# Softmax denominators of an attention stage: 32x32 transposes and column halvings in place of products with ones

## The chip, the cores and the metric

The kernel runs on one core of a Trainium2 chip. The metric is the device time of one execution in microseconds (us). Engines: TensorE (PE; its weight loads are PEld), VectorE (DVE), ScalarE (ACT), GpSimd (POOL) and SyncE (SP), which issues most transfers. Each runs its own instructions in order, and they wait for one another by semaphores.

## The reference

Four stages over 4 sequences of 1024 rows of 256 values: a mixing attention, an expert layer, causal attention with 16 heads of 64, and the expert layer again. The change is in the causal attention:

```python
q = jnp.einsum('ntc,hdc->nhtd', x_q, w_q)
k = jnp.einsum('ntc,hdc->nhtd', x_q, w_k)
v = jnp.einsum('ntc,hdc->nhtd', x_q, w_v)
a = jnp.einsum('nhtd,nhsd->nhts', q, k) / math.sqrt(q.shape[3])
a = jnp.where(causal_forbidden[None, None], -jnp.inf, a)
a = jax.nn.softmax(a, axis=3)
y = jnp.einsum('nhts,nhsd->nthd', a, v).reshape(a.shape[0], t, -1)
return y @ w_o
```

## The kernel before

**Units and iterations.** Attention works through 32 units u (4 sequences times 8 pairs of heads). A unit has two chunks c of 512 queries. Chunk 0 has key tiles kt 0 to 3, chunk 1 kt 0 to 7 (128 keys each), so a unit is six iterations of two key tiles: two for chunk 0, four for chunk 1. `attend(u)` writes them out and hands over, at numbered places, to the work of the next unit (projections, row maxima), which the engines take in between. The order on each engine is the order of this text.

**What a key tile passes through.** PE multiplies keys and queries into two PSUM banks, one for each head (`high_scores` L1411, `scores` L1427). ACT takes the exponential into a buffer `t_p` (L1713; there are four). On the diagonal POOL zeroes the forbidden half (`affine_select`, L2370; the mask). One iteration later PE multiplies the weights with the values (`weigh` L1446, both heads into bank 6), and POOL adds the tile to the chunk's sum `t_acc` (`add_up` L2390, 128 keys x 2 heads x 512 queries; L2387 copies what the next tile leaves out). `weigh` of a diagonal tile waits for its mask. ACT copies the finished sum of values to `t_pvs` (L1731).

**The denominators.** `t_acc` still has to be summed over its 128 partitions. `divide` (L1456) multiplies it with 64 columns of ones, 512 columns a head, so that 64 partitions a head hold the same denominators. `sum_rows` on DVE transposes that bank in 32x32 blocks (L2204), inverts one column of each block (L2206), and `scale_rows` turns the inverses back to rows (L2213); POOL multiplies them into `t_pvs` and writes `t_yT` (L2404), which the output products (L1471) read. The chunk that ended with iteration n-3 is divided in `finish(n)`, ahead of that iteration's `weigh`, and scaled one iteration later. So chunk 1 of unit u-1 is divided in iteration 2 of unit u (below: den A), and chunk 0 of unit u in iteration 4 (den B). The first sum of a chunk in the next unit waits until PE has read the old one.

**Row maxima of the next unit.** PE multiplies whole blocks (`row_max` L1376, L1389) and DVE takes the maxima (`part_max` L2180 with the mask, L2186 without), which frees the banks. Seven banks go round in turn (`work_ring`) for scores, maxima, projections and denominators; PE takes a bank only when it has been drained. In iteration 1 DVE has masked maxima of 384 and 512 columns, then in iteration 2 of 128 and 256, then plain ones of 512 in two lots of four, one of them at the end of iteration 3.

Of the kernel before, what the change touches and what calls it, by code (L numbers as in the profile page):

```python
# [15 lines left out]
P = 128  # L16
# [32 lines left out]
class Kernel:  # L49
# [34 lines left out]
    def semaphores(self):  # L84
# [38 lines left out]
        self.pe_pv, self.a_pvs, self.p_yt = s("pe_pv"), s("act_pvs"), s("pool_yT")  # L123
        self.d_den = Marks(s("dve_den"), "reciprocal", "rows")

# [14 lines left out]
    def constant_tiles(self, st):  # L140
# [105 lines left out]
    def attention_tiles(self, st):  # L246
# [35 lines left out]
        t["wo"] = sb("t_wo", [P, NHP, D])  # L282
        t["den"] = [sb("t_den", [P, BANK]) for _ in range(2)]
        t["rden"] = [sb("t_rden", [P, BANK // 32]) for _ in range(2)]
# [107 lines left out]
class Program:  # L392
# [30 lines left out]
    xt_block = qk_load = v_load = qk_product = qk_low = qk_double = v_product = skip  # L423
    row_max = part_max = max_rows = high_scores = scores = weigh = add_up = divide = sum_rows = scale_rows = skip
    values_done = out_weights = out_load = out_product = out_add = skip
# [303 lines left out]
    def attention(self):  # L729
# [77 lines left out]
        def sums(n, *tiles):  # L807

            if 0 < n <= len(pairs):
                u, c, kt = pairs[n - 1]  # L810
                for i in tiles:
                    self.add_up(u, c, kt + i)

        def finish(n):

            if ends(n - 3):
                self.divide(*pairs[n - 3][:2])
            if 0 < n <= len(pairs):
                u, c, kt = pairs[n - 1]
                self.weigh(u, c, kt)  # L820
                self.weigh(u, c, kt + 1)
            if ends(n - 3):
                self.sum_rows(*pairs[n - 3][:2])
            if ends(n - 4):
                scale(*pairs[n - 4][:2])
# [135 lines left out]
        def units():  # L961
# [60 lines left out]
class TensorE(Program):  # L1022
# [711 lines left out]
class VectorE(Reader):  # L1734

    def constants(self):
# [453 lines left out]
    def max_rows(self, u):  # L2190
# [4 lines left out]
        dve.tensor_scalar(t["neg"][u % 2][:], k.bank[bank][0:2 * k.NBLK, 0:P], -1.0, None, ALU.mult).then_inc(k.drained[bank], 1)  # L2195

    def sum_rows(self, u, c):
# [3 lines left out]
        den = t["den"][c]  # L2201
# [3 lines left out]
        self.wait_drained(("den", u, c))  # L2205
        dve.reciprocal(t["rden"][chunk % 2][:, :], den[:].rearrange("p (n j) -> p n j", j=32)[:, :, 0]  # L2206
                       ).then_inc(k.d_den.sem, 1)

    def scale_rows(self, u, c):
        k, dve, t = self.k, self.e, self.k.t  # L2210
        chunk = 2 * u + c
        self.wait_ge(k.d_den.sem, k.d_den.at(chunk, "reciprocal"))
        dve.transpose(t["den"][c][:], spread(t["rden"][chunk % 2][:], 2, 32)).then_inc(k.d_den.sem, 1)  # L2213

# [8 lines left out]
class GpSimd(Reader):  # L2223
# [149 lines left out]
    def add_up(self, u, c, kt):  # L2373
# [16 lines left out]
        pool.tensor_tensor(acc[:, :, q0:], (p0 if kt == 1 else acc)[:, :, q0:], p[:, :, q0:],  # L2390
                           ALU.add).then_inc(k.p_acc, 1)

    def scale_rows(self, u, c):
# [10 lines left out]
        pool.tensor_tensor(t["yT"][c][:, hp, :], t["pvs"][chunk % 2][:], t["den"][c][:],  # L2404
                           ALU.mult).then_inc(k.p_yt, 1)
# [236 lines left out]
```

## Time and profile before

| | us |
|---|---|
| median of 3 runs (2241.84 to 2243.07) | 2243.05 |
| span of the profiled execution | 2235.8 |
| PE busy | 2149.9 (96%) |
| DVE busy | 1465.4 (66%) |
| POOL busy | 1368.7 (61%) |
| attention stage, from its first unit to its last den | 644 to 1804 |

The span runs from the first to the last instruction; 7.25 us lie around it. The busy share of an engine is a mean over stages. In the timelines a row is a start, a duration, an engine, a line and an operation with the tiles that it writes and reads; in brackets stands how long the engine had been idle, and for whom. A duration of PE is modelled and overlaps the next one, so the work of PE is better read from starts and from the chain of waits.

### The profile page before, as it was taken

The page shows a single profiled execution, that of the slowest core. Times are in us where ns is not written, and L with a number is a line of the kernel's source. Part 1 is how long each engine was busy: PE and PEld are TensorE (multiplying, and loading weights), DVE is VectorE, ACT ScalarE, POOL GpSimd, SP SyncE. Part 2 cuts the span into 40 slices and gives each one's busy share as a digit, 9 for nine tenths or more (in the row PEclk, how much of TensorE's full clock was granted, in tenths as well). Part 3 has the DMA queues.
Part 4 walks back from the last instruction along what each step waited for, and adds up shares of the span by engine and source line. Part 5 has one row for each costly group of instructions (what it writes and reads, how often), then busy time and mean ns, then how long its engine had stood idle before and what let it go on. Part 6 is the DMA issues. An engine that isn't in the chain of part 4 may idle for free.

```text
span 2235.8 us, 34077 instructions
## 1 busy us (share of the span) xinstructions
PE 2149.9 (96%) x12130; PEld 1597.8 (71%) x12130; DVE 1465.4 (66%) x3349; ACT 1003.6 (45%) x1907; POOL 1368.7 (61%) x1237
## 2 busy tenths in 40 slices
PE   6998999999999999999999999999999899999997
PEld 5455788889876666766657666667666588889997
DVE  6365688675757666467674577874877636975553
ACT  4411553444445545345553354542554425434443
POOL 2322676677537776566674576664677846777774
PEclk9899999999999999999999999999999999999999
DMA  4432544555432212212312222221220244545552
GB/s 132 144 129 86 151 117 111 151 144 137 114 88 67 51 36 76 67 52 73 76 48 67 67 78 56 58 61 54 76 76 21 76 132 115 140 113 139 134 144 29
DMA packets 145048, 206.04 MB, mean 92 GB/s; under 512 B 19432, under 2 KB 112112, under 8 KB 144880
## 3 DMA queue, kind: packets, MB, share of 16 engines
q1 hardware_dynamic: 120304, 170.30, 25.4%
q0 software_dynamic: 24576, 33.57, 8.8%
q8 instruction: 97, 1.59, 0.3%
q14 instruction: 71, 0.58, 0.1%
HBM read 130.03 MB, written 39.85 MB: 76 GB/s over the span
## 4 chain that ended last, share of the span: by engine, by line
PE 73%; DVE 9%; issue 4%; POOL 4%; ACT 2%; DMA 1%; SPq 1%; POOLq 0%; DVEq 0%; ACTq 0%
PE psum L1299 12%; PE psum L1320 11%; PE psum L1446 11%; PE psum L1348 7%; PE psum L1411 7%; PE psum L1427 6%; PE psum L1471 5%; PE psum L1362 4%; PE psum L1376 3%; PE psum L1456 3%; POOL t_acc L2390 2%; DVE f_hlo L2134 1%; DVE f_hhi L2132 1%; PE psum L1389 1%; PE psum L1267 1%
## 5 line engine op out<-in xcount | busy, mean ns | idle before, releaser
L1713 ACT ACTIVATE t_p<-psum 128x512 f32<-128x512 f32 (+3 forms) x768 | 323.6, 492 | 294.3 <-PE psum L1427 284.6
L2390 POOL TENSOR_TENSOR t_acc<-t_acc,t_p 128x1024 f32<-128x1024 f32 (+3 forms) x256 | 416.9, 1629 | 14.5 <-ACT t_p L1713 0.5
L2309 POOL TENSOR_TENSOR f_wlo<-f_wst,f_whi 128x256 fp32r<-128x256 f32 x256 | 221.8, 922 | 150.6 <-ACT f_whi L1646 150.6
L1320 PE MATMUL psum<-f_whi,f_hhi 128*128 128x256 f32 x1024 | 294.9, 288 | 6.2 <-DVE f_hlo L2134 6.1
L1446 PE MATMUL psum<-t_p,t_v 128*64 128x512 f32 (+3 forms) x1536 | 288.8, 496 | 7.3 <-POOL t_p L2370 7.3
L1320 PE MATMUL psum<-f_whi,f_hlo 128*128 128x256 f32 x1024 | 289.4, 283 | 0.0
L1320 PE MATMUL psum<-f_wlo,f_hhi 128*128 128x256 f32 x1024 | 289.2, 282 | 0.0
L2132 DVE CAST f_hhi<-f_h 128x512 fp32r<-128x512 f32 x256 | 141.9, 554 | 208.0 <-ACT f_h L1664 153.2
L1664 ACT ACTIVATE f_h<-psum 128x512 f32<-128x512 f32 x256 | 153.0, 598 | 275.8 <-PE psum L1299 246.8
L1411 PE MATMUL psum<-t_qa,t_ka 128*128 128x512 f32 (+3 forms) x768 | 222.7, 370 | 1.8 <-DVE t_mx L2180 0.6
L2390 POOL TENSOR_TENSOR t_acc<-t_p 128x768 f32<-128x768 f32 x64 | 134.6, 2103 | 136.4 <-PE psum L1456 133.1
L1446 PEld LDWEIGHTS psum<-t_p,t_v 128*64 128x64 f32 x1536 | 98.9, 137 | 161.8 <-issue 143.8
L2370 POOL TENSOR_SCALAR_AFFINE_SELECT t_p<-t_p 128x256 f32<-128x256 f32 x256 | 105.0, 420 | 175.0 <-ACT t_p L1713 174.5
L1299 PE MATMUL psum<-f_xhi,f_whi 128*128 128x512 f32 x512 | 204.8, 400 | 7.4 <-DVE f_xlo L2118 3.8
L1427 PE MATMUL psum<-t_qb,t_kb 65*128 65x512 f32 (+3 forms) x768 | 205.8, 349 | 4.9 <-DMA t_qb<-t_neg 4.5
L2134 DVE TENSOR_TENSOR f_hlo<-f_h,f_hhi 128x512 fp32r<-128x512 f32 x256 | 200.3, 783 | 8.8
L1320 PEld LDWEIGHTS psum<-f_whi,f_hhi 128*128 128x128 f32 x1024 | 194.9, 190 | 15.0 <-DVE f_hlo L2134 8.1
L1299 PE MATMUL psum<-f_xlo,f_whi 128*128 128x512 f32 x512 | 201.9, 394 | 0.0
L1299 PE MATMUL psum<-f_xhi,f_wlo 128*128 128x512 f32 x512 | 200.9, 392 | 0.0
L1320 PEld LDWEIGHTS psum<-f_wlo,f_hhi 128*128 128x128 f32 x1024 | 195.2, 191 | 4.8
L1320 PEld LDWEIGHTS psum<-f_whi,f_hlo 128*128 128x128 f32 x1024 | 195.0, 190 | 0.0
L2186 DVE TENSOR_REDUCE t_mx<-psum 128x1 f32<-128x512 f32 x256 | 159.6, 683 | 41.5 <-PE psum L1376 38.9
(288 smaller groups left out, 4408.1 us busy)
## 6 DMA issues: line engine op xcount, KB each, us to landing
f_wst<-in_L_ffn_w SPq DMA_DIRECT2D x64, 1024.0 KB
t_ka<-t_ka SPq DMA_DIRECT2D x64, 256.0 KB, 3.3
t_qb<-t_qa SPq DMA_DIRECT2D x64, 256.0 KB, 4.0
t_wk<-wkT SPq DMA_DIRECT2D x32, 256.0 KB, 4.0
t_wq<-wqT SPq DMA_DIRECT2D x32, 256.0 KB, 4.0
t_wv<-wvT SPq DMA_DIRECT2D x16, 512.0 KB, 4.9
normal<-f_xy SPq DMA_DIRECT2D x5, 1024.0 KB, 10.3
a_x<-in_L_attn_a_x SPq DMA_DIRECT2D x4, 1024.0 KB, 10.0
```

What stands on the lines that cost most here:

```text
L1299: m = pe.matmul(k.bank[b], w[:, dt, fs], x[:, dt, :], start=(dt == 0 and j == 0), stop=(dt == k.DT - 1 and j == 2))
L1320: m = pe.matmul(out, h[:, js], w[:, f, :], start=(f == 0 and a == 0 and j % 2 == 0), stop=(f == FT - 1 and a == 2), skip_group_check=True)
L1348: m = pe.matmul(k.bank[bank], w[:, part, ct, :], x[:, ct, cs], start=(ct == 0 and a == 0), stop=(ct == 1 and a == 2))
L1411: pe.matmul(k.bank[bank][:, q0:], hd["ka"][:, ks], hd["qa"][:, qs], start=True, stop=False)
L1427: pe.matmul(k.bank[banks[i]][:, q0:], hd["kb"][0:k.QROWS, ks], hd["qb"][0:k.QROWS, qs], start=False, stop=True).then_inc(k.filled[banks[i] ...
L1446: m = pe.matmul(k.bank[6][i * DH:(i + 1) * DH, q0:BANK], v[:, kt, vs:vs + DH], p[:, i, q0:BANK], start=(kt == 0), stop=(kt == last), skip_ ...
L1713: act.activation(p[:, i, q0:], k.bank[bank][:, q0:], ACT.Exp, scale=1.0 / float(np.sqrt(k.DH))).then_inc(k.drained[bank], 1)
L2132: dve.tensor_copy(hhi[:], h[:]).then_inc(k.d_h.sem, 1)
L2134: dve.tensor_tensor(hlo[:], h[:], hhi[:].bitcast(F32), ALU.subtract).then_inc(k.d_h.sem, 1)
L2186: s = dve.tensor_reduce(mx1[:, i, n - k.KPC:n - k.KPC + 1], part, AX.X, ALU.max)
L2309: m = pool.tensor_tensor(t["wlo"][n % 2][:, i, ks], t["wst"][:, i, ks], t["whi"][n % 2][:, i, ks].bitcast(F32), ALU.subtract)
L2390: pool.tensor_tensor(acc[:, :, q0:], (p0 if kt == 1 else acc)[:, :, q0:], p[:, :, q0:], ALU.add).then_inc(k.p_acc, 1)
```

## The change

The partition sum is made in three steps. `fold_sums` on DVE transposes the whole sum `t_acc`, 128 x 1024, in 32x32 blocks into a new tile `t_turned`; now each partition holds, for one query of a block, 32 keys in 32 columns. `fold_sums` on POOL adds these 32 columns in five halvings in place (16, 8, 4, 2 and 1 columns of each of the 32 blocks), the last into `t_part` (128 x 32); each waits for the one ahead of it. `divide` then multiplies `t_part` with `fold` (a matrix that adds the four groups of 32 partitions), 16 columns a head, and DVE inverts those 16 columns straight out of PSUM. The rows of inverses go into one half of `t_turned`, so the tile is shared: DVE may turn a new sum into it only once POOL has multiplied with the last rows (`p_yt`).

The order changes as well: `fold_sums` stands at the start of the iteration, and `divide` behind that iteration's `weigh`.

```diff
@@ tiles
-        t["den"] = [sb("t_den", [P, BANK]) for _ in range(2)]
+        t["turned"] = sb("t_turned", [P, 2 * BANK])
+        t["den"] = [t["turned"][:, c * BANK:(c + 1) * BANK] for c in range(2)]
+        t["part"] = sb("t_part", [P, 2 * BANK // 32])
@@ attention()
+        def fold(n):
+            if ends(n - 3):
+                self.fold_sums(*pairs[n - 3][:2])
         def finish(n):
-            if ends(n - 3):
-                self.divide(*pairs[n - 3][:2])
             if 0 < n <= len(pairs):
                 u, c, kt = pairs[n - 1]
                 self.weigh(u, c, kt)
                 self.weigh(u, c, kt + 1)
             if ends(n - 3):
+                self.divide(*pairs[n - 3][:2])
                 self.sum_rows(*pairs[n - 3][:2])
@@ attend(u)
+                fold(n)
                 sums(n, 0)
@@ TensorE.divide
-        self.wait_ge(k.p_acc, k.sum_count(u, c, k.KPC * (c + 1) - 1))
+        self.wait_ge(k.p_fold, 5 * (2 * u + c + 1))
         for i in range(2):
-            m = pe.matmul(k.bank[bank][i * DH:(i + 1) * DH, :], k.ones[:, 0:DH], t["acc"][(2 * u + c) % 2][:, i, :],
+            m = pe.matmul(k.bank[bank][i * DH:(i + 1) * DH, 0:n], k.fold[:], t["part"][:, i * n:(i + 1) * n],
@@ VectorE
+    def fold_sums(self, u, c):
+        self.wait_ge(k.p_acc, k.sum_count(u, c, k.KPC * (c + 1) - 1))
+        if chunk:
+            self.wait_ge(k.p_yt, chunk)
+            self.wait_filled(("den", (chunk - 1) // 2, (chunk - 1) % 2))
+        dve.transpose(t["turned"][:], t["acc"][c][:].rearrange("p i q -> p (i q)")).then_inc(k.d_den.sem, 1)
     def sum_rows(self, u, c):
-        if chunk > 1:
-            self.wait_ge(k.p_yt, chunk - 1)
-        dve.transpose(den[:], k.bank[bank]).then_inc(k.drained[bank], 1)
-        dve.reciprocal(t["rden"][chunk % 2][:, :], den[:].rearrange("p (n j) -> p n j", j=32)[:, :, 0]
+        dve.reciprocal(t["rden"][chunk % 2][:, :], k.bank[bank][:, 0:BANK // 32]).then_inc(k.drained[bank], 1)
@@ GpSimd
     def add_up(self, u, c, kt):
             if u:
-                self.wait_filled(("den", u - 1, c))
+                self.wait_ge(k.d_den.sem, k.d_den.at(2 * (u - 1) + c, "turned"))
+    def fold_sums(self, u, c):
+        rows = t["turned"][:].rearrange("p (n j) -> p n j", j=32)
+        self.wait_ge(k.d_den.sem, k.d_den.at(chunk, "turned"))
+        if chunk:
+            self.wait_filled(("den", (chunk - 1) // 2, (chunk - 1) % 2))
+        for n, w in enumerate((16, 8, 4, 2, 1)):
+            if n:
+                self.wait_ge(k.p_fold, 5 * chunk + n)
+            out = rows[:, :, 0:w] if w > 1 else t["part"][:].unsqueeze(2)
+            pool.tensor_tensor(out, rows[:, :, 0:w], rows[:, :, w:2 * w], ALU.add).then_inc(k.p_fold, 1)
```

The order on POOL from the scaling of chunk 1 of the last unit (`t_yT`) to that of chunk 0, iterations 3 to 5. First before, then with the change:

```order
L2390 TENSOR_TENSOR t_acc<-t_p 128x1024
L2404 TENSOR_TENSOR t_yT<-t_pvs,t_den 128x512
L2390 TENSOR_TENSOR t_acc<-t_acc,t_p 128x1024
L2370 AFFINE_SELECT t_p<-t_p 128x2x128 x2
L2390 TENSOR_TENSOR t_acc<-t_acc,t_p 128x1024 x2
L2370 AFFINE_SELECT t_p<-t_p 128x2x128 x2
L2390 TENSOR_TENSOR t_acc<-t_acc,t_p 128x2x384
L2404 TENSOR_TENSOR t_yT<-t_pvs,t_den 128x512
```

```order
L2437 TENSOR_TENSOR t_yT<-t_pvs,t_turned 128x512
L2424 TENSOR_TENSOR t_turned<-t_turned 128x32x16
L2424 TENSOR_TENSOR t_turned<-t_turned 128x32x8
L2424 TENSOR_TENSOR t_turned<-t_turned 128x32x4
L2424 TENSOR_TENSOR t_turned<-t_turned 128x32x2
L2424 TENSOR_TENSOR t_part<-t_turned 128x32
L2409 TENSOR_TENSOR t_acc<-t_acc,t_p 128x1024
L2389 AFFINE_SELECT t_p<-t_p 128x2x128 x2
L2409 TENSOR_TENSOR t_acc<-t_acc,t_p 128x1024 x2
L2389 AFFINE_SELECT t_p<-t_p 128x2x128 x2
```

The five additions stand ahead of one sum and of the masks (`AFFINE_SELECT`) of key tiles 4 and 5, and so ahead of those of 6 and 7.

The order on DVE in iterations 3 and 4, from the way back of the inverses (`t_rden`) to the next inversion. First before, then with the change:

```order
L2213 STREAM_TRANSPOSE t_den<-t_rden 128x512
L2186 TENSOR_REDUCE t_mx_142<-psum 128x1 x4
L2180 ISA psum,t_mx<-psum,t_mask,t_mx_142 128x256
L2180 ISA t_mx 128x1
L2180 ISA psum,t_mx<-psum,t_mask,t_mx_142 128x256
L2180 ISA t_mx 128x1
L2204 STREAM_TRANSPOSE t_den<-psum 128x512
L2206 RECIPROCAL t_rden<-t_den 128x16
```

```order
L2232 STREAM_TRANSPOSE t_turned<-t_rden 128x512
L2200 TENSOR_REDUCE t_mx_143<-psum 128x1 x4
L2219 STREAM_TRANSPOSE t_turned<-t_acc 128x1024
L2194 ISA psum,t_mx<-psum,t_mask,t_mx_143 128x256
L2194 ISA t_mx 128x1
L2194 ISA psum,t_mx<-psum,t_mask,t_mx_143 128x256
L2194 ISA t_mx 128x1
L2225 RECIPROCAL t_rden<-psum 128x16
```

The turn of the sum stands behind the four plain maxima of 512 columns. In iteration 2 it stands in the same way behind the masked maxima of 512 columns, at the end of iteration 1.

The order on PE in iteration 4, around den B. First before, then with the change:

```order
L1411 MATMUL psum<-t_qa,t_ka 128x384 x2
L1427 MATMUL psum<-t_qb,t_kb 128x384 x2
L1456 MATMUL psum<-t_acc,ones 64x512 x2
L1446 MATMUL psum<-t_p,t_v 64x512 x4
L1376 MATMUL psum<-t_ka,t_qa 128x384 x2
```

```order
L1422 MATMUL psum<-t_qa,t_ka 128x384 x2
L1438 MATMUL psum<-t_qb,t_kb 128x384 x2
L1457 MATMUL psum<-t_p,t_v 64x512 x4
L1468 MATMUL psum<-t_part,fold 64x16 x2
L1387 MATMUL psum<-t_ka,t_qa 128x384 x2
```

The products of the denominators have moved behind the products with the values, and have 16 columns for 512.

## Rows read from the trace of the kernel before

**Rows 1.** The page, busy time by engine

```profile
PE 2149.9 (96%) x12130; PEld 1597.8 (71%) x12130; DVE 1465.4 (66%) x3349; ACT 1003.6 (45%) x1907; POOL 1368.7 (61%) x1237
```

**Rows 2.** The table by stretch, attention stage: PE, PEld, DVE, ACT, POOL, clock

```profile
644.00:1807.00 1163.00, 1145.38 (x6178) 755.86 (x6177) 780.17 (x1996) 559.52 (x1190) 750.45 (x679) 0.99 0.23 61
```

**Rows 3.** The chain of work around unit 11: start, duration, what

```profile
1045.97 1.01 PE psum L1456 x4
1046.98 0.65 PE psum L1446 x8
...
1064.39 0.79 PE psum L1221 x8
```

**Rows 4.** The timeline of PE, units 12 and 13: start, duration, what

```profile
1080.50 1.08 PE L1456 MATMUL psum<-t_acc,ones 128*64 128x512 f32 x4
...
1086.97 0.74 PE L1376 MATMUL psum<-t_ka,t_qa 64*128 64x512 f32 x4
...
1089.72 1.08 PE L1456 MATMUL psum<-t_acc,ones 128*64 128x512 f32 x4
...
1097.51 0.87 PE L1446 MATMUL psum<-t_p,t_v 128*64 128x256 f32 x8
...
1112.84 1.08 PE L1456 MATMUL psum<-t_acc,ones 128*64 128x512 f32 x4
...
1135.49 0.70 PE L1427 MATMUL psum<-t_qb,t_kb 65*128 65x512 f32 x2 [2.22 <-DMA t_qb<-t_neg]
...
1146.86 1.08 PE L1456 MATMUL psum<-t_acc,ones 128*64 128x512 f32 x4
```

**Rows 5.** The timeline of DVE in the same units

```profile
1087.51 2.48 DVE L2186 TENSOR_REDUCE t_mx<-psum 128x1 f32<-128x512 f32 x4 [1.17 <-PE psum L1376]
...
1109.86 0.73 DVE L2180 CUSTOM_DVE_ANT_0 psum<-psum,t_mask 128x512 f32<-128x512 f32 x1
...
1145.88 0.73 DVE L2180 CUSTOM_DVE_ANT_0 psum<-psum,t_mask 128x512 f32<-128x512 f32 x1
```

**Rows 6.** Groups on POOL by form: xcount, busy us, mean ns, idle before

```profile
L2390 POOL TENSOR_TENSOR t_acc<-t_acc,t_p 128x1024 f32<-128x1024 f32 x96 | 227.4, 2369 | 5.3 <-ACT t_p L1713 0.5 <-POOL t_acc L2390 0.4
...
L2390 POOL TENSOR_TENSOR t_acc<-t_acc,t_p 128x512 f32<-128x512 f32 x64 | 83.3, 1301 | 4.4
...
L2390 POOL TENSOR_TENSOR t_acc<-t_acc,t_p 128x256 f32<-128x256 f32 x64 | 47.0, 734 | 4.7
...
L2279 POOL TENSOR_TENSOR b_rstd<-b_rstd,minus_half 128x2 f32<-128x2 f32 x8 | 5.6, 698 | 36.6 <-DVE b_rstd L1882 36.5
```

**Rows 7.** Groups on DVE by form, the same columns

```profile
L2204 DVE STREAM_TRANSPOSE t_den<-psum 128x512 f32<-128x512 f32 x64 | 45.9, 717 | 34.8 <-PE psum L1456 31.3
...
L2213 DVE STREAM_TRANSPOSE t_den<-t_rden 128x512 f32<-128x512 f32 x64 | 45.0, 703 | 0.0
...
L1987 DVE STREAM_TRANSPOSE f_turned<-f_ind 128x32 f32<-128x32 f32 x30 | 6.4, 212 | 1.0
```

**Rows 8.** The timeline of POOL, unit 12 and the start of 13

```profile
1086.41 1.28 POOL L2404 TENSOR_TENSOR t_yT<-t_pvs,t_den 128x512 f32<-128x512 f32 x1 [2.31 <-DVE t_den L2213]
1087.65 2.38 POOL L2390 TENSOR_TENSOR t_acc<-t_acc,t_p 128x1024 f32<-128x1024 f32 x1
...
1091.03 4.87 POOL L2390 TENSOR_TENSOR t_acc<-t_acc,t_p 128x1024 f32<-128x1024 f32 x2
1095.85 0.76 POOL L2370 TENSOR_SCALAR_AFFINE_SELECT t_p<-t_p 128x256 f32<-128x256 f32 x2
...
1108.36 2.16 POOL L2390 TENSOR_TENSOR t_acc<-t_acc,t_p 128x512 f32<-128x512 f32 x2
1114.08 2.37 POOL L2390 TENSOR_TENSOR t_acc<-t_p 128x1024 f32<-128x1024 f32 x1 [3.56 <-PE psum L1456]
```

**Rows 9.** The table by stretch, behind a stall of PE: the columns of rows 2

```profile
1135.00:1139.00 4.00, 3.51 (x12) 2.99 (x13) 2.82 (x4) 2.33 (x5) 1.83 (x4) 0.75 0.52 131
1139.00:1143.00 4.00, 4.00 (x20) 2.83 (x20) 2.03 (x4) 3.42 (x9) 1.91 (x5) 0.82 0.00 0
```

More of the change, by code:

```diff
@@ L123, in semaphores @@
         self.pe_pv, self.a_pvs, self.p_yt = s("pe_pv"), s("act_pvs"), s("pool_yT")
-        self.d_den = Marks(s("dve_den"), "reciprocal", "rows")
+        self.d_den = Marks(s("dve_den"), "turned", "rows")
+        self.p_fold = s("pool_fold")
         self.q_x, self.q_w1, self.q_w2, self.q_gate = s("loaded_x"), s("loaded_w1"), s("loaded_w2"), s("loaded_gate")
@@ L146, in constant_tiles @@
         self.minus_half = c("minus_half", [P, self.NBLK])
+        self.fold = c("fold", [P, self.DH])
         self.NCAND = 8
@@ L423 @@
     xt_block = qk_load = v_load = qk_product = qk_low = qk_double = v_product = skip
-    row_max = part_max = max_rows = high_scores = scores = weigh = add_up = divide = sum_rows = scale_rows = skip
+    row_max = part_max = max_rows = high_scores = scores = weigh = add_up = skip
+    fold_sums = divide = sum_rows = scale_rows = skip
     values_done = out_weights = out_load = out_product = out_add = skip
@@ L1004, in units @@
             for n in range(4):
+                fold(len(pairs) + n)
                 sums(len(pairs) + n, 0, 1)
@@ L1452, in divide @@
         DH = k.DH
+        n = BANK // 32
         bank = self.take(("den", u, c), self.work_bank())
-        self.wait_ge(k.p_acc, k.sum_count(u, c, k.KPC * (c + 1) - 1))
+        self.wait_ge(k.p_fold, 5 * (2 * u + c + 1))
         for i in range(2):
-            m = pe.matmul(k.bank[bank][i * DH:(i + 1) * DH, :], k.ones[:, 0:DH], t["acc"][(2 * u + c) % 2][:, i, :],
+            m = pe.matmul(k.bank[bank][i * DH:(i + 1) * DH, 0:n], k.fold[:], t["part"][:, i * n:(i + 1) * n],
                           start=True, stop=True, skip_group_check=True)
@@ L1741, in constants @@
                           ALU.max).then_inc(k.d_const, 1)
+        for n in range(0, k.DH, 32):
+            dve.tensor_reduce(k.fold[:, n:n + 32], k.ident[:].rearrange("p (g d) -> p d g", d=32), AX.X, ALU.add)
         dve.tensor_copy(k.tokid[:], k.tok_i[:])
@@ L2195, in max_rows @@
         dve.tensor_scalar(t["neg"][u % 2][:], k.bank[bank][0:2 * k.NBLK, 0:P], -1.0, None, ALU.mult).then_inc(k.drained[bank], 1)
+    def fold_sums(self, u, c):
+        k, dve, t = self.k, self.e, self.k.t
+        chunk = 2 * u + c
+        self.wait_ge(k.p_acc, k.sum_count(u, c, k.KPC * (c + 1) - 1))
[3 more added lines that the diff above has]
+        dve.transpose(t["turned"][:], t["acc"][c][:].rearrange("p i q -> p (i q)")).then_inc(k.d_den.sem, 1)
     def sum_rows(self, u, c):
@@ L2200, in sum_rows @@
         bank = self.wait_filled(("den", u, c))
-        den = t["den"][c]
-        if chunk > 1:
-            self.wait_ge(k.p_yt, chunk - 1)
-        dve.transpose(den[:], k.bank[bank]).then_inc(k.drained[bank], 1)
-        self.wait_drained(("den", u, c))
-        dve.reciprocal(t["rden"][chunk % 2][:, :], den[:].rearrange("p (n j) -> p n j", j=32)[:, :, 0]
-                       ).then_inc(k.d_den.sem, 1)
+        dve.reciprocal(t["rden"][chunk % 2][:, :], k.bank[bank][:, 0:BANK // 32]).then_inc(k.drained[bank], 1)
     def scale_rows(self, u, c):
@@ L2211, in scale_rows @@
         chunk = 2 * u + c
-        self.wait_ge(k.d_den.sem, k.d_den.at(chunk, "reciprocal"))
-        dve.transpose(t["den"][c][:], spread(t["rden"][chunk % 2][:], 2, 32)).then_inc(k.d_den.sem, 1)
+        self.wait_drained(("den", u, c))
+        self.wait_ge(k.p_fold, 5 * (chunk + 1))
+        dve.transpose(t["den"][c], spread(t["rden"][chunk % 2][:], 2, 32)).then_inc(k.d_den.sem, 1)
     def out_add(self, b, c, n):
@@ L2391, in add_up @@
                            ALU.add).then_inc(k.p_acc, 1)
+    def fold_sums(self, u, c):
+        k, pool, t = self.k, self.e, self.k.t
+        chunk = 2 * u + c
+        rows = t["turned"][:].rearrange("p (n j) -> p n j", j=32)
[7 more added lines that the diff above has]
+            pool.tensor_tensor(out, rows[:, :, 0:w], rows[:, :, w:2 * w], ALU.add).then_inc(k.p_fold, 1)
     def scale_rows(self, u, c):
@@ L2403, in scale_rows @@
         self.wait_ge(k.a_pvs, chunk + 1)
-        pool.tensor_tensor(t["yT"][c][:, hp, :], t["pvs"][chunk % 2][:], t["den"][c][:],
+        pool.tensor_tensor(t["yT"][c][:, hp, :], t["pvs"][chunk % 2][:], t["den"][c],
                            ALU.mult).then_inc(k.p_yt, 1)
```

## The prediction

> **What bounds the kernel now.** I read the page's first part first: PE is busy for 96% of the span [rows 1]. The table by stretch says the same of attention, where the change is: 1145 us of 1163, with DVE at 780 and POOL at 750 [rows 2]. So PE sets the time, and two thirds of the time of DVE and POOL is taken too. Then the timeline of PE. In it a unit is as rigid as a clock: den A to den A takes 32.3 us (1080.50 to 1112.84), den B comes 9.22 us behind den A, and the weighing of key tiles 6 and 7 starts 17.0 us behind it (1097.51) [rows 4]. The 31 distances from den A to den A between 688.12 and 1803.94 are 29.5 to 46.2 us; in 23 of them the weighing of tiles 6 and 7 comes at +17.0, in three at +17.7, in two at +19.2, in three at +30.8.
> Last, the timelines of DVE and POOL, to see who works shortly ahead of PE. DVE ends the masked maxima of iteration 1 at 1110.59, 2.25 us ahead of den A, and in the next unit at 1146.61, 0.25 us ahead [rows 4, 5]. POOL ends mask 6 at about 1096.25 (half of the 0.76 us from 1095.85), 1.25 us ahead of PE [rows 4, 8]. Neither costs anything, and neither has much to spare.
>
> **What PE gives back.** The chain shows 1.01 us for a den and 0.65 us for the weighing behind den A [rows 3]. The new den has as many products and weight loads, but 16 columns. The nearest row is the eight small products of L1221 (8 columns), 0.79 us [rows 3]; four of them are 0.40 us. Saved: 0.61 us a den, 64 x 0.61 = 39 us. Were the new den as dear as the old, it would be 0; were it free, 65.
>
> **What is added.** DVE turns 1024 columns. 32 columns take 212 ns and 512 take 703 [rows 7], which is 1.02 ns a column, so 1024 take 0.703 + 512 x 0.00102 = 1.23 us, in place of the 0.717 us from PSUM that goes. POOL's five additions put out 512, 256, 128, 64 and 32 columns. The rows for 512 and 256 are 1.301 and 0.734 us; 256 to 1024 give 2.13 ns a column and 0.19 us fixed, so the others take 0.46, 0.33 and 0.26: 3.08 us [rows 6]. Each waits for the one ahead of it. Two sums in a row that do so take 4.87 us where two alone take 4.74 [rows 8, 6], so 0.13 us a wait, four of them 0.52. **One fold on POOL is 3.6 us**, two a unit. From below it is 3.1 (no price on the waits), from above 4.7 (the three small ones as dear as L2279, 2 columns for 0.698 us [rows 6]; that is another operation, so I stay with the line through the same one). POOL's load in attention becomes 750 + 64 x 3.6 = 980 of 1163 us, DVE's about 810. Neither becomes the bound by its load. What counts is where the fold stands in the chain.
>
> **Den A.** The sum is long done, so DVE turns it as soon as its maxima of iteration 1 are through: end of these, 1.23 of DVE, 3.6 of POOL and 0.1 between them, 4.95 us. PE comes 0.65 us later than before, since it weighs first. With DVE's end 2.25 us ahead [rows 4, 5] the stall is 4.95 - 2.25 - 0.65 = 2.05 us; with 0.25 ahead it is 4.05. Over the 31 units DVE's end lies 0.1 to 6.3 us ahead of den A; six units have no stall, the others 1.2 to 4.2, together 60 us. Behind the waiting den on PE stand the row maxima for which DVE waits, so neither runs ahead meanwhile.
>
> **Den B.** Count from the start of den A, time 0. Before, the second lot of plain maxima is multiplied at +6.47 (1086.97) and reduced by DVE from +7.01 to +9.49 [rows 4, 5]. With the change PE is 0.61 + 0.65 earlier there (cheaper den, weighing already done), so DVE ends them at +8.2. Only then comes the turn: +9.5. POOL has by then added its three sums (2.16 and 2.37 [rows 8]) and multiplied t_yT, and stands idle. Fold: to +13.1. PE wanted den B at 9.22 - 1.26 + 1.7 (the weighing now ahead of it) = +9.7, so it waits 3.4 us. But the later end is POOL's: before, t_yT ended at +7.2 and POOL then ran without a gap, one sum, masks 4 and 5, two sums, to the end of mask 6 at +15.75 [rows 8], 8.6 us. With the change these 8.6 us begin at +13.1: mask 6 at +21.6. PE would be ready at 17.0 - 2 x 0.61 - 0.65 = +15.1. **The two waits of PE in this stretch come to 6.5 us** in the 23 units with +17.0, 5.7 in three, 4.3 in two; in the three with +30.8 other work of PE covers the mask and I put 1 us for den B. Together 149 + 17 + 9 + 3 = 178 us, and 6 for the first unit. What is late next is nothing: POOL has caught up with the diagonal of the next unit, whose mask before waited for ACT.
>
> **The clock.** Behind a stall of 2.22 us (before 1135.49) the granted clock fell from full to half for part of the next eight microseconds: 0.75 and 0.82 in two stretches of 4 us [rows 4, 9], which is 4 x 0.25 + 4 x 0.18 = 1.7 us lost. Behind den A nothing covers this; 11 of its stalls are longer than 2.2 us: 19 us. Behind den B the wait for the mask covers it.
>
> **Sum.** -39 + 60 + 178 + 6 + 19 = +224. The span becomes 2235.8 + 224 = 2459.8, with the 7.25 us around it 2467. The constants (two reductions of 32 columns ahead of the first barrier) are under 1 us.
>
> **Rivals.**
> *Covered (faster).* The idle time of POOL takes the fold: 3.56 us before the first sum of chunk 1, for den A, and 2.31 before t_yT [rows 8], 5.9 us a unit, and 7.2 are added. Then only PE's gain is left: 2243 - 39 = 2204. It turns on one place, the end of mask 6: it has 1.25 us to spare, and the faster PE takes 1.9 of them back, so any delay there costs, and from about 2.5 us a unit on the gain is gone. Against it: both idle times lie ahead of t_yT, the second fold behind it, where POOL had no gap.
> *One wait only.* PE stalls at den A, but the second fold finds cover, because DVE, idle during the first stall, works ahead. 2243 - 39 + 60 + 19 = 2283. Against it: the maxima ahead of the second turn need products that PE makes behind den A.
> *Dear halvings.* Runs of 16 to 1 columns cost more than long rows. At half as much again for each of the 992 columns, 992 x 2.13 x 0.5 = 1.06 us a fold, which the other bound above (4.7) gives too. It counts in some 56 places: 2467 + 59 = 2526. No row here has a sum over such short runs. The Trainium skill, GPSIMD Engine Reference, section "Performance pitfalls for Q7 kernels", says that reads with a step of over 8 bytes take about half as much time again for an element. By the letter the rule bears on the last halving alone, whose step is 128 bytes, and the sum would be 2467 plus 2 us; read as a rule on short runs it is this rival. No row here shows such a read.
> *The change does nothing.* The new waits eat just what PE gives back, 2243: needs 0.6 us of stall a den, a tenth of what the rows give.
>
> **How the numbers follow.** Forecast as summed 0.60; dear halvings 0.14; one wait only 0.13; covered 0.06; within 0.2% 0.02; worse than all of these, with the clock at half for long stretches, 0.05. The forecast's own range is 2400 to 2510: 3.1 us for a fold takes 27 us off, DVE nearer to PE in the late units another 30 to 40, and half a microsecond more in a fold adds 28. The range from the case of one wait to that of dear halvings is 2275 to 2550, and leaves out 0.06, 0.02 and 0.05. The change is measured to about 0.2%, 4.5 us, so faster has 0.06, same 0.02, slower 0.92.
>
> **What the profile of the changed kernel would show.** PE's den at about 0.4 us, the turn at 1.23, the five additions at 3.1 summed and 3.6 from first start to last end. PE idle ahead of den A and den B with POOL's fold as the releaser, and ahead of the weighing of tiles 4 and 6 with the mask. Mask 6 at +21.6 behind den A. A den A to den A of about 39 us where it was 32.3. POOL idle between t_yT and the second fold, waiting for the turn. The time outside attention unchanged. It is wrong if PE's waits for masks stay at a few microseconds in all, or if DVE's turn of chunk 0 ends well ahead of +9.5.

## The result and the profile after

The changed kernel takes **2456.98 us** (2456.03 to 2460.86, 4 runs) and the one before, on the same chip, 2242.45 (2241.39 to 2243.07). The ratio is 1.096 (95% interval 1.095 to 1.098): **slower by 214.5 us**. The forecast was 2467, with a range of 2275 to 2550. It was near, and yet two terms of its sum were off, in opposite directions; that they cancel is luck.

The page of the changed kernel, busy time by engine and the shares of the chain of waits by engine:

```profile
PE 2216.0 (90%) x12130; PEld 1638.9 (67%) x12130; DVE 1510.1 (62%) x3351; ACT 1007.1 (41%) x1907; POOL 1557.6 (63%) x1557
...
PE 49%; DVE 16%; POOL 15%; issue 6%; ACT 4%; DMA 1%; SPq 1%; another core or an unknown queue 0%; POOLq 0%; DVEq 0%; ACTq 0%
```

The span is 2454.5 us. No engine is fuller than 90%, and PE's share of the chain that ends last has fallen to half (73% on the page of before): the chain now changes engines. The table by stretch (stretch and length, then PE, PEld, DVE, ACT, POOL, granted clock), attention stage:

```profile
640.00:2024.00 1384.00, 1216.54 (x6215) 802.49 (x6214) 822.75 (x1998) 566.62 (x1196) 942.90 (x1002) 0.91 0.19 52
```

Against [rows 2] PE was idle for 18 us and is now for 167. The stages ahead of attention are as they were, and from the last den to the end of the span it is 432 us in both kernels. All of the loss is in attention. PE's busy time rose as well, by 71 us, although its products became smaller, and the clock is 0.91 where it was 0.99.

The groups of attention that the change touches (shapes apart; busy, mean ns | idle before <-releaser), which answer to [rows 6, 7]:

```profile
L2219 DVE STREAM_TRANSPOSE t_turned<-t_acc 128x1024 f32<-128x1024 f32 x64 | 79.2, 1238 | 5.0 <-POOL t_acc L2409 3.8 <-POOL t_yT L2437 1.2
...
L2424 POOL TENSOR_TENSOR t_turned<-t_turned 128x512 f32<-128x512 f32 x64 | 81.9, 1279 | 272.0 <-DVE t_turned L2219 272.0
L2424 POOL TENSOR_TENSOR t_turned<-t_turned 128x256 f32<-128x256 f32 x64 | 46.2, 722 | 5.0
L2424 POOL TENSOR_TENSOR t_turned<-t_turned 128x128 f32<-128x128 f32 x64 | 29.1, 455 | 5.0
L2424 POOL TENSOR_TENSOR t_turned<-t_turned 128x64 f32<-128x64 f32 x64 | 18.8, 294 | 5.0
L2424 POOL TENSOR_TENSOR t_part<-t_turned 128x32 f32<-128x32 f32 x64 | 15.4, 240 | 5.0
...
L1468 PE MATMUL psum<-t_part,fold 128*64 128x16 f32 x256 | 19.7, 221 | 130.7 <-POOL t_part L2424 130.7
```

The turn is 1.24 us. The five additions sum to 2.99, and each of the four that wait for the one ahead lost 5.0 / 64 = 0.08 us: a fold is 3.3 us. POOL stands idle for 272 us until DVE has turned, and PE for 130.7 until POOL has folded. The waits of the stage, those of PE and the longest of the others (total, times, longest):

```profile
POOL t_turned L2424 <- DVE t_turned L2219: 272.0, 63, 8.5
ACT t_p L1725 <- POOL t_acc L2409: 178.3, 36, 9.3
...
PE psum L1468 <- POOL t_part L2424: 130.7, 54, 3.9
...
PE psum L1457 <- POOL t_p L2389: 23.7, 32, 3.1
```

PE waits little for masks (L1457). Why that does not clear them shows in one of the light units, with den A at 779.60. First PE and then POOL around its den B:

```profile
779.60 0.29 PE L1468 MATMUL psum<-t_part,fold 128*64 128x16 f32 x4 [0.85 <-POOL t_part L2424]
...
792.32 0.29 PE L1468 MATMUL psum<-t_part,fold 128*64 128x16 f32 x4 [3.00 <-POOL t_part L2424]
...
795.16 3.25 PE L1457 MATMUL psum<-t_p,t_v 128*64 128x512 f32 x8
...
800.71 0.87 PE L1457 MATMUL psum<-t_p,t_v 128*64 128x256 f32 x8
```

```profile
788.89 2.97 POOL L2424 TENSOR_TENSOR t_turned<-t_turned 128x512 f32<-128x512 f32 x4 [3.53 <-DVE t_turned L2219]
791.94 0.24 POOL L2424 TENSOR_TENSOR t_part<-t_turned 128x32 f32<-128x32 f32 x1
792.13 2.36 POOL L2409 TENSOR_TENSOR t_acc<-t_acc,t_p 128x1024 f32<-128x1024 f32 x1
794.45 0.77 POOL L2389 TENSOR_SCALAR_AFFINE_SELECT t_p<-t_p 128x256 f32<-128x256 f32 x2
795.19 4.85 POOL L2409 TENSOR_TENSOR t_acc<-t_acc,t_p 128x1024 f32<-128x1024 f32 x2
799.99 0.77 POOL L2389 TENSOR_SCALAR_AFFINE_SELECT t_p<-t_p 128x256 f32<-128x256 f32 x2
```

PE waits 3.00 us for the fold. Behind that it runs at half clock: the weighing of tiles 4 and 5 takes 3.25 us where it takes 1.72 at full clock, and so PE comes to the weighing of tiles 6 and 7 at 800.71, 0.34 us behind the end of mask 6 (799.99 and half of 0.77), and shows no wait. The mask sets the time, but the slow clock has taken the place of the wait for it. In [rows 4] this weighing came 17.0 us behind den A; now it is 21.1.

The chain of waits through the next unit (start, duration, what) goes once around the engines for each den:

```profile
813.12 1.11 DVE t_turned L2219
814.30 1.29 POOL t_turned L2424
...
817.38 0.25 POOL t_part L2424
817.77 0.29 PE psum L1468 x4
...
822.88 0.44 PE psum L1387
823.95 1.88 DVE t_mx L2200 x3
825.83 1.16 DVE t_turned L2219
827.06 1.28 POOL t_turned L2424
...
830.11 0.25 POOL t_part L2424
830.50 0.40 PE psum L1468 x4
```

Den A is released by turn and fold, then PE multiplies for the maxima of L1387, DVE reduces these and turns only then, POOL folds, and den B is released.

### The profile page after: what moved, and what is told of

The parts are those of the page before. It is cut to its first block, busy times and chain, and to the rows that moved or that the text cites. A ratio compares the mean times of both kernels' runs of the same rounds, so it can differ in the third digit from the quotient of the medians.

```text
span 2454.5 us, 34502 instructions
## 1 busy us (share of the span) xinstructions
PE 2216.0 (90%) x12130; PEld 1638.9 (67%) x12130; DVE 1510.1 (62%) x3351; ACT 1007.1 (41%) x1907; POOL 1557.6 (63%) x1557
## 4 chain that ended last, share of the span: by engine, by line
PE 49%; DVE 16%; POOL 15%; issue 6%; ACT 4%; DMA 1%; SPq 1%; another core or an unknown queue 0%; POOLq 0%; DVEq 0%; ACTq 0%
PE psum L1310 10%; PE psum L1331 10%; PE psum L1457 6%; POOL t_turned L2424 6%; POOL t_acc L2409 6%; PE psum L1483 5%; PE psum L1359 4%; PE psum L1422 4%; PE psum L1438 3%; DVE t_turned L2219 3%; DVE t_mx L2200 2%; PE psum L1387 2%; ACT t_p L1725 2%; DVE t_qa L2178 2%; DVE psum L2194 2%
## 5 line engine op out<-in xcount | busy, mean ns | idle before, releaser
L1457 PE MATMUL psum<-t_p,t_v 128*64 128x512 f32 (+3 forms) x1536 | 347.2, 579 | 23.7 <-POOL t_p L2389 23.7
L2424 POOL TENSOR_TENSOR t_turned<-t_turned 128x512 f32<-128x512 f32 (+3 forms) x256 | 176.0, 687 | 287.1 <-DVE t_turned L2219 272.0
L1422 PE MATMUL psum<-t_qa,t_ka 128*128 128x512 f32 (+3 forms) x768 | 239.1, 394 | 1.9 <-DVE e_Rw L2092 1.3
L1457 PEld LDWEIGHTS psum<-t_p,t_v 128*64 128x64 f32 x1536 | 104.2, 153 | 188.6 <-issue 126.2
L1438 PE MATMUL psum<-t_qb,t_kb 65*128 65x512 f32 (+3 forms) x768 | 223.1, 375 | 5.2 <-DMA t_qb<-t_neg 5.2
L2347 POOL DMA_INDIRECT f_xg<-normal,f_idx x128 | 134.8, 1053 | 59.8 <-issue 41.9
```

The lines of the kernel that those rows point to most:

```text
L1422: pe.matmul(k.bank[bank][:, q0:], hd["ka"][:, ks], hd["qa"][:, qs], start=True, stop=False)
L1438: pe.matmul(k.bank[banks[i]][:, q0:], hd["kb"][0:k.QROWS, ks], hd["qb"][0:k.QROWS, qs], start=False, stop=True).then_inc(k.filled[banks[i] ...
L1457: m = pe.matmul(k.bank[6][i * DH:(i + 1) * DH, q0:BANK], v[:, kt, vs:vs + DH], p[:, i, q0:BANK], start=(kt == 0), stop=(kt == last), skip_ ...
L2424: pool.tensor_tensor(out, rows[:, :, 0:w], rows[:, :, w:2 * w], ALU.add).then_inc(k.p_fold, 1)
```

## Experiments

Distances from den A to den A and on to den B are read from the starts of L1468 (or what stands in its place) in PE's timeline, over the same 31 units in each kernel. In us, where "light" is a unit without other work, as at 1080 in [rows 4]:

| kernel | ratio to before | sum of 31 distances | light unit | den A to den B, sum |
|---|---|---|---|---|
| before | 1 | 1115.8 | 32.3 | 299 |
| small product alone | 0.981 | 1072.8 | 30.9 | 276 |
| fold of one addition | 1.024 | 1165.2 | 33.8 | 316 |
| five additions for den A, one for den B | 1.069 | 1270.5 | 34.9 | 366 |
| five for den B, one for den A | 1.062 | 1246.7 | 37.3 | 396 |
| full fold, PE does not wait for it | 1.061 | 1245.9 | 37.2 | 318 |
| the change | 1.096 | 1322.3 | 38.1 | 437 |
| the change, fill at den A | 1.081 | 1287.7 | 38.0 | 397 |
| the change, fill at both | 1.086 | 1301.2 | 37.9 | 395 |

**1. The small product alone.** The kernel before, with 16 of the 512 columns multiplied and inverted; the denominators of the others are left out.

```diff
-            m = pe.matmul(k.bank[bank][...], k.ones[:, 0:DH], t["acc"][...][:, i, :],
+            m = pe.matmul(k.bank[bank][..., 0:16], k.ones[:, 0:DH], t["acc"][...][:, i, 0:16],
-        dve.transpose(den[:], k.bank[bank]).then_inc(k.drained[bank], 1)
-        dve.reciprocal(t["rden"][chunk % 2][:, :], den[:].rearrange(...)[:, :, 0])
+        dve.reciprocal(t["rden"][chunk % 2][:, :], k.bank[bank][:, 0:16])
```

> The kernel before with the product over ones cut to 16 columns a head, inverted straight out of PSUM; nothing turned, nothing folded, order and waits as before (the other 496 columns of denominators are left out). It shows what PE gives back when nobody waits for more. By my sum 39 us: 2204 us, den A to den B 8.6 us. If the columns cost nothing, because PE is held by the waits of others, 2240.

Measured: 2197.45 us against 2239.14, ratio 0.981 (0.979 to 0.982), 42 us gained. This is all that PE gives back, and what the change could have brought with a free fold.

**2. A fold of one addition.** One halving instead of five; the other columns of each block are left out.

```diff
-        for n, w in enumerate((16, 8, 4, 2, 1)):
+        for n, w in enumerate((1,)):
```

> The changed kernel with one addition on GpSimd in place of five (columns 0 and 1 of each block; 30 of the 32 columns are left out of the sum, the rest is as it was). The turn on DVE, the waits and the order stay. If the place of the fold in the chain is what costs: the fold falls from 3.3 us (first start to last end in the trace of the changed kernel) to about 0.3; den A waits only in the units in which DVE is late, den B no more (turn at +9.5, PE wants it at +9.7), but mask 6 still comes at about +18.5 where PE is ready at +15.1, since GpSimd stands idle until the turn: 2243 - 39 + 4 + 88 = about 2300 us, den A to den B 9.7 us. If the clock or the load of the turn on DVE is what costs, the time stays above 2380.

Measured: 2294.05 against 2239.14, ratio 1.024 (1.022 to 1.026). The longest waits of PE in attention:

```profile
PE psum L1457 <- POOL t_p L2389: 75.6, 54, 5.4
PE psum L1483 <- POOL t_yT L2437: 3.1, 3, 2.0
PE psum L1468 <- POOL t_part L2424: 2.7, 4, 0.8
```

PE hardly waits for the dens (2.7 us), and still the kernel is slower than before: the turn behind the maxima, with all that POOL queues behind it, delays the masks by more than PE had gained.

**3. Full fold, and PE does not wait for it.** Turn and fold run as in the change, but PE multiplies 16 columns of `t_acc` itself; the fold's result is left out of the denominators. POOL's first sum of a chunk waits once more until PE has read the old one, which costs POOL 1.5 us in all.

```diff
-        self.wait_ge(k.p_fold, 5 * (2 * u + c + 1))
+        self.wait_ge(k.p_acc, k.sum_count(u, c, k.KPC * (c + 1) - 1))
-            m = pe.matmul(..., k.fold[:], t["part"][:, i * n:(i + 1) * n],
+            m = pe.matmul(..., k.ones[:, 0:DH], t["acc"][c][:, i, 0:n],
```

> The changed kernel in which DVE turns and GpSimd folds as they do, but PE's small product reads the sum itself (16 columns a head, as in the kernel before with a small product) and does not wait for the fold; the denominators of the other columns are left out. If late masks are a cost of their own: mask 6 still ends at about +20.8 and PE stands ahead of the weighing of tiles 6 and 7: 2350 to 2400 us, den A to den B 9.7. If the waits at den A and den B are the whole cost, the time falls to 2204 to 2230.

Measured: 2377.39, ratio 1.061 (1.059 to 1.063). Its longest wait of PE:

```profile
PE psum L1457 <- POOL t_p L2389: 109.4, 46, 3.7
```

With PE's waits for the dens gone, that for the masks rises from 23.7 to 109.4 us, and a light unit still takes 37.2 us of 38.1. The masks wait behind the fold in POOL's queue, and this costs without any wait for a den. In a light unit mask 6 ends 20.7 us behind den A, where it ends 15.0 us behind it with the small product alone.

**4. The fold behind the masks on POOL.** The five additions stand behind the masks of their iteration.

```diff
                 self.scores(u, c, kt + 1)
+                halve(n)
                 sums(n, 1)
```

> The changed kernel with the five additions on GpSimd moved behind the first sum and the two masks of their iteration. GpSimd no longer stands idle for the turn (3.5 us a unit), so mask 6 comes at +19.0 in place of +20.8; den B comes later, +13.7 for +12.7. If the mask alone bound the unit, 1.7 us a unit would be gained, 2405. If, as I think, the later den B and the half clock behind it bind together with the mask, 0.5 us or less a unit: 2435 to 2457.

Measured: 2439.99 against 2233.73, ratio 1.091 (1.089 to 1.093). PE waits for masks 3.1 us (23.7 in the change) and for dens 138.7 (130.7). Mask 6 ends earlier, 17.8 us behind den A in the light units for 20.8, and still the weighing of tiles 6 and 7 starts at 19.6 to 21.0 there (20.9 to 21.4 in the change): den B comes at +12.7 as before, and with the masks early it is den B and the slow products behind it that hold PE. Half a per cent is all that the order on POOL brings. The expectation had mask 6 at +19.0 and den B at +13.7, both about 1 us late; the time is in its band.

**5. Which den costs more.** Five additions for one den of a unit and one for the other (the columns of the shorter fold are left out).

```diff
-        for n, w in enumerate((16, 8, 4, 2, 1)):
+        for n, w in enumerate((16, 8, 4, 2, 1) if c == 1 else (1,)):
```

> The changed kernel with five additions for chunk 1 (den A) and one for chunk 0 (den B, where 30 of 32 columns are left out). Against the kernel with one addition for both, 2294 us, only den A's fold is 3 us longer. By my sum the stalls at den A were 60 us, of which 4 stand in that kernel already, and 19 us of clock behind the long ones: 2294 + 56, and up to 75: 2350 to 2369 us.

> The reverse: five additions for chunk 0 (den B), one for chunk 1. Against 2294 us, masks 4 to 7 and den B come 3 us later in some 28 units: 2294 + 84 = 2378 us, 2365 to 2395. If this and the reverse kernel together add more than the changed kernel has over 2294 us (163 us), the two folds cover each other in part; if less, they make each other worse.

Measured: den A alone 2394.34 (2381 to 2396) against 2233.95, ratio 1.069 (1.066 to 1.073), a miss by 25 us; den B alone 2372.78, ratio 1.062 (1.060 to 1.064), as expected. Over the fold of one addition, a ratio point being 22.4 us, den A's four additions cost 101 us and den B's 84, together 185; in the full change it is 162, so the two cover 23 us of each other. Den A's share had been sized at 56 to 75 us. The trace shows what was missed. PE waits 45 us more ahead of den A than with one addition, and the way from den A to den B, on which nothing of den A's fold lies, grew by 50 us in sum. In the unit with den A at 1134.04 it is 9.68 us; in that with den A at 1055.41 it is 12.74:

```profile
1055.41 0.29 PE L1468 MATMUL psum<-t_part,fold 128*64 128x16 f32 x4 [2.56 <-POOL t_part L2424]
1055.64 1.22 PE L1387 MATMUL psum<-t_ka,t_qa 64*128 64x512 f32 x4
1056.79 1.22 PE L1422 MATMUL psum<-t_qa,t_ka 128*128 128x512 f32 x2
...
1060.93 2.65 PE L1457 MATMUL psum<-t_p,t_v 128*64 128x512 f32 x8
...
1134.04 0.29 PE L1468 MATMUL psum<-t_part,fold 128*64 128x16 f32 x4 [0.73 <-POOL t_part L2424]
1134.27 0.73 PE L1387 MATMUL psum<-t_ka,t_qa 64*128 64x512 f32 x4
1134.93 0.73 PE L1422 MATMUL psum<-t_qa,t_ka 128*128 128x512 f32 x2
```

Behind the stall of 2.56 us the same four products take 1.22 us, not 0.73. The granted clock from 1058 to 1062 in that kernel (clock in the third column from the end) is half:

```profile
1058.00:1062.00 4.00, 4.00 (x13) 2.35 (x13) 2.21 (x7) 2.17 (x4) 2.96 (x2) 0.50 0.03 6
```

These slow products are the ones whose maxima DVE takes ahead of the next turn. This points to a price of the clock behind den A, and experiments 6 and 7 take its measure.

**6. A first fill, which ran over.** Unused products of 512 columns ahead of PE's waits, 2 at den A and 7 at den B; nothing is left out.

```diff
+        for n_ in range(2 if c else 7):
+            pe.matmul(k.bank[bank][0:DH, :], k.ones[:, 0:DH], t["wo"][:, 0:2, :]...)
         self.wait_ge(k.p_fold, 5 * (2 * u + c + 1))
```

> The changed kernel with products of 512 columns that nothing uses, put ahead of PE's wait for the fold: two (about 0.85 us) at den A, seven (about 3.0 us) at den B, so that PE works where it stood idle. If the half clock behind the stalls is merely covered by the wait for the mask: the granted clock of the attention stage rises from 0.91 to near 0.98 and the time stays within 25 us of the changed kernel, 2432 to 2460. If the half clock is itself the main cost (285 us of the stage stand at half clock, up to 140 us of work), the time falls to 2350 or less.

Measured: 2467.82, ratio 1.101 (1.099 to 1.103), slower than the change and above the band of either theory. The clock was 0.99 in attention, as wanted. But one of these products is two passes, together 0.86 us, and the fill is longer than the wait:

```profile
788.18 5.74 PE L1467 MATMUL psum<-t_wo,ones 128*64 128x512 f32 x13
```

That is 5.7 us where PE had waited 3.0. The way from den A to den B became 489 us in sum, for 437 in the change, so the overrun hides whatever the clock gave back, and this run does not show what the slow clock costs.

**7. Fills to measure.** Products of 256 columns, as many as the idle time of each den in the trace of the change holds: 0 to 9 at den A, 6 at den B (none in the units in which PE did not wait there). One kernel has both fills, the other that at den A alone; nothing is left out. `fill` is the table of counts.

```diff
+        for _ in range(fill[c][u]):
+            pe.matmul(k.bank[bank][0:DH, 0:256], k.ones[:, 0:DH], t["wo"][:, 0, :], ...)
         self.wait_ge(k.p_fold, 5 * (2 * u + c + 1))
```

> The same, with the fill at den A alone; the 3.0 us waits at den B stay empty, and the clock may fall behind them. Nothing is left out. Theory A: what the half clock costs it costs behind den A, since behind den B the wait for mask 6 covers it: 2405 to 2430, at most 15 us above the kernel with both fills. Theory B: 2438 or a little above. If the half clock behind den B costs as well (it reaches past mask 6 into the next den A), this kernel is 20 us or more above the one with both fills.

> The changed kernel with unused products of 256 columns (two passes, 0.43 us at full clock) ahead of each wait of PE for a den, this time as many as its own idle times in the trace of the change hold: at den A 0 to 9 a unit (idle of that unit over 0.43, rounded down), at den B 6 (2.6 of the 3.0 us), none where PE had no idle time. The earlier filled kernel had put 5 to 6 us of products ahead of a 3.0 us wait and 1.7 ahead of 0.85, so it overran and could not price the clock. Nothing is left out. Theory A, read from the trace of the change and of the fold at den A alone: where the stall at den A is 1.45 us or more the clock is at half for about 8 us behind it, the products for the maxima ahead of the turn of chunk 0 come 3.2 us later, and den B and mask 6 with them; over all units 42 us. With the clock kept up den A to den B is 12.7 us in every unit and the time is 2457 - 42 = 2415, 2395 to 2425. Theory B, as forecast: the half clock costs 19 us in all: 2438. Theory C, all of it is covered: 2450 to 2465.

Measured, both beside 2235.5 of before: the fill at den A alone 2417.13, ratio 1.081 (1.079 to 1.083); both fills 2428.12, ratio 1.086 (1.084 to 1.088), 3 us outside its band and 11 us slower than the one with fewer. The bands were counted from the change at 2457, whose kernel before took 2242; by the ratios the two kernels stand at 2423 and 2435 on that scale. The first is as theory A said. The second is near the 2438 of theory B, so its time alone does not decide between the two; the way from den A to den B does, which both fills shorten alike. Against the change the fill at den A gives back 1.0964 - 1.0807, or 35 us by the ratios, and also 35 by the trace (1322.3 to 1287.7 in the table). The way from den A to den B falls from 437 to 397 us in sum: 12.7 in every unit but those with other work. This one is shown: **the half clock behind den A costs 35 to 40 us**, since the fill stands only where PE had been idle. The unit of the change with den A at 1076.35 and the same one with the fill; first the change:

```profile
1076.35 0.40 PE L1468 MATMUL psum<-t_part,fold 128*64 128x16 f32 x4 [1.72 <-POOL t_part L2424]
1076.68 1.22 PE L1387 MATMUL psum<-t_ka,t_qa 64*128 64x512 f32 x4
...
1093.56 0.40 PE L1468 MATMUL psum<-t_part,fold 128*64 128x16 f32 x4 [2.88 <-POOL t_part L2424]
```

```profile
1066.83 0.29 PE L1471 MATMUL psum<-t_part,fold 128*64 128x16 f32 x4 [0.76 <-POOL t_part L2427]
1067.05 0.74 PE L1387 MATMUL psum<-t_ka,t_qa 64*128 64x512 f32 x4
...
1079.56 0.30 PE L1471 MATMUL psum<-t_part,fold 128*64 128x16 f32 x4 [3.00 <-POOL t_part L2427]
```

17.2 us between the dens have become 12.7. At den B the fill gives nothing back. With that wait filled too, PE is fast until it meets the mask, waits there, and the clock falls behind that. The waits of PE, first with the fill at den A alone, then with both:

```profile
PE psum L1471 <- POOL t_part L2427: 91.0, 46, 3.0
PE psum L1457 <- POOL t_p L2392: 14.7, 16, 2.2
```

```profile
PE psum L1457 <- POOL t_p L2392: 74.8, 55, 5.4
PE psum L1471 <- POOL t_part L2427: 18.5, 45, 3.0
```

In a light unit that is equal (38.0 and 37.9 us). In the unit around 1189 it is not: 44.1 us with both fills, 41.9 with one. With both, the clock is at half from 1213 to 1221, 24 us behind den A, where ACT twice waits 1.67 us for PE's projections (L1359); with one it was at half 12 to 20 us behind den A, where PE would have waited for the mask anyway. This was read from the one unit. In others the difference has either sign, and where the rest of the 11 us comes from is not shown; den B itself comes no later (395 and 397 us in the table).

**8. The 32 columns added on DVE.** One reduction in place of the five additions, right behind the turn.

```diff
         dve.transpose(t["turned"][:], t["acc"][c][:]...).then_inc(k.d_den.sem, 1)
+        self.wait_ge(k.d_den.sem, k.d_den.at(chunk, "turned"))
+        dve.tensor_reduce(t["part"][:], t["turned"][:].rearrange("p (n j) -> p n j", j=32), AX.X, ALU.add)
```

> The changed kernel with the 32 columns summed by one reduction on DVE behind its turn (128x1024 to 128x32, about 1.1 us by the 0.68 us of a reduction of 512 columns), nothing on GpSimd. If the serial 3.3 us on GpSimd ahead of the masks is what costs: masks come as before the change, den B waits 1 us (turn and sum end at +10.7, PE wants them at +9.7), den A in the units in which DVE is late: 2243 - 39 + 34 + 11 = 2249, up to 2290 if DVE, with 3.5 us more a unit, falls behind elsewhere. If DVE's load is what costs: above 2320.

Measured: 2260.66 against 2233.73, ratio 1.012 (1.010 to 1.014). The reduction takes 1.22 us, where POOL's fold takes 3.3, and POOL's queue is free of it:

```profile
L2221 DVE TENSOR_REDUCE t_part<-t_turned 128x32 f32<-128x1024 f32 x64 | 78.1, 1220 | 2.2
```

It takes away seven eighths of the loss (from 9.6% to 1.2%). In a light unit mask 6 ends 14.3 us behind den A (20.8 in the change), and the unit takes 32.35 us, as before. The fold is shorter here as well as out of POOL's queue, and this run does not separate the two. It is still slower than before: turn and reduction stand 2.5 us long behind the maxima, and PE waits 33.2 us for them, 25.0 of it at den B.

**9. The product kept, in one pass.** The kernel before, with `t_acc` written as fp32r and multiplied with a band of zeros and ones, so that the two heads add up in one bank.

```diff
-        t["acc"] = [sb("t_acc", [P, 2, BANK]) for _ in range(2)]
+        t["acc"] = [sb("t_acc", [P, 2, BANK], F32R) for _ in range(2)]
-            m = pe.matmul(k.bank[bank][i * DH:(i + 1) * DH, :], k.ones[:, 0:DH], t["acc"][...][:, i, :],
+            m = pe.matmul(k.bank[bank], t["band"][:, (1 - i) * DH:(3 - i) * DH], t["acc"][...][:, i, :],
```

> The kernel before with its product over ones in the rounded type fp32r: the sums t_acc are written as fp32r by GpSimd, and a band of 64 zeros, 64 ones and 64 zeros gives both heads their 64 partitions out of one pass each (two products of 512 columns in place of four records). Nothing else moves. A product of 512 columns in this type takes 0.23 us in the chain of the kernel before (six of L1348 1.39 us), so a den falls from 1.01 to 0.46 or to 0.61 us: 25 to 35 us gained, 2208 to 2218, den A to den B about 8.7 us. If GpSimd writes the rounded type more slowly (a split of 256 columns takes 0.92 us where a sum takes 0.73), masks come late and the gain is gone: 2240 to 2290.

Measured: 2215.32 (2212.28 to 2218.52) against 2233.73, ratio **0.992** (0.990 to 0.993): 0.8% faster than the kernel before, and clear of its interval. The gain of 18 us is below the 25 to 35 expected, although the time lies in the band, which was counted from 2243. Den A to den B in a light unit is 8.83 us (9.22 before, 8.7 expected), 0.39 a den. It takes from PE a part of what the change wanted to take, 18 of 42 us, and adds nothing to anybody's queue.

## Why the prediction was near, and where it was wrong

One ratio point is 22.4 us here, and a difference of two kernels is uncertain by some 5 us.

| term | forecast | measured | from |
|---|---|---|---|
| PE gives back | -39 | -44 | small product alone |
| den B, masks, first unit | +184 | +181 | PE does not wait, over small product |
| stalls at den A | +60 | +44 | fill at den A, over PE does not wait |
| half clock | +19 | +35 | the change, over fill at den A |
| sum | +224 | +216 | |

The rows are differences of neighbouring kernels, so they add up to the whole by construction; what each stands for is read from the traces and not shown by the sum. In the second row only 109 us are idle time of PE ahead of masks, where the forecast had all of it as waiting. The granted clock of that kernel from the first den A to the last is 0.93 (0.99 with the small product alone), so slow products fill a part of the way to the mask, as they do in the change.

- **PE's gain** was a little small because the new den is 0.29 us at full clock, and 0.40 was taken from [rows 3]; at half clock it is 0.40.
- **The fold** is 3.3 us where 3.6 was forecast: additions 2.99 (3.08) and 0.08 a wait (0.13). The turn is 1.24 (1.23).
- **Den B and masks** went as worked out: the second turn ends at +9.2 in the light unit with den A at 817.77 (825.75 + 1.23 in DVE's timeline), forecast +9.5; PE waits 3.0 us (3.4); mask 6 ends at +20.8 (+21.6). A light unit takes 38 us, forecast 39. The point on which it turned, that the turn of chunk 0 finds DVE busy with maxima that PE makes behind den A, stands in the chain. What I had not seen is that PE's own wait for den B costs nothing beyond the mask: without it a light unit is just the 0.85 us shorter that PE waits at den A.
- **Stalls at den A** were too large: 44.8 us of idle time in 31 units, not 60. The shorter fold explains 25 x 0.3 = 8 of these 15, and the rest is open.
- **The clock is the step that failed.** I took one fall from [rows 4, 9], 1.7 us, times 11 long stalls, and added it where it stands. It is larger and works at a distance: in the unit at 1076.35 den B comes 4.5 us later, because what PE does at half clock is the product for which DVE, and then the turn, waits. Nor was the length of a stall the mark. Behind one of 2.55 us (den A at 1790.8) the granted clock stayed at 1.00 until 1800, and the way to den B at 12.7; behind one of 1.06 us (1122.2) it was 0.76 and then 0.50 up to 1130, and the way grew by 3.2. What decides between these two is open. Behind den B my reason, that the wait for the mask covers it, held in the light units (38.0 and 37.9 us with that wait empty and filled); to keep the clock up there did not make the kernel faster but 11 us slower.

The rivals: *covered* and *one wait only* fall with the waits of PE, 3.0 us at nearly every den B. Of *the change does nothing* I had written that it needs a tenth of the stalls of the rows; 0.6 us is a sixth of the 3.7 a den that they give. *Dear halvings* falls by the groups above: 0.240 us for 32 columns, where the line through 1024 to 256 gives 0.26. The Trainium skill, GPSIMD Engine Reference, section "Performance pitfalls for Q7 kernels", asks half as much time again for an element at steps over 8 bytes. The last halving reads at steps of 128 bytes and shows no such surcharge; on 32 columns it would be 0.03 us, so this is a weak trial of the rule. Expected and seen only in a small part: PE idle ahead of the weighing, 23.7 us in all, where 3.1 us a unit were forecast. As a sign of being wrong, waits for masks of "a few microseconds" would have misled, for slow products hid most of them.

ACT's 178.3 us of waiting for `t_acc` to free its buffers, up to 9.3 at a time, I had not forecast. Whether it adds to the loss apart from the masks, whose queue is the same, was not tried.

## What to carry over

Before work is moved off the busiest engine, walk the chain that results around all engines: 42 us of PE's time were bought with a turn and a fold that stand between two lots of PE's own products, twice a unit, and ahead of masks in POOL's queue that they have nothing to do with. A cheaper form of the same step on the same engine (0.992 here) puts nothing into anybody's queue. And a stall has two prices, its own length and the slow products behind it; whether the second counts depends on who waits for these products.

## What the runs showed of the hardware that I had not expected

- POOL's additions over runs of 16 to 1 columns with gaps cost as long rows do: 512, 256, 128, 64 and 32 results in 1.279, 0.722, 0.455, 0.294 and 0.240 us. One that waits for the one ahead starts 0.08 us after its end.
- DVE adds 1024 columns in groups of 32 in 1.22 us, as long as it takes to transpose them (1.24).
- PE busier can be slower: with the fill at den B added to that at den A (504 records of unused products for 180), the granted clock from 640 to 2000 us rose from 0.93 to 0.96 and the kernel lost 11 us. In the unit that was followed the slow stretch had only moved to a place where it is waited for.
